# Third-norm cluster logits: the row block as stationary side, the centroids as 128 and 64 moving columns

## The reference, cut to what matters

```
x = x + 0.5 * ffn(layernorm(x))
x = x + attention(layernorm(x))
x = x + 0.5 * ffn(layernorm(x))

def ffn(x):                                   # x: 4096 x 1024
    dots = softmax(x @ centroids.T / 0.1)     # 64 centroids of 1024 features
    hits = dots > 0.01
    query_sel   = any(hits, axis=1)           # per token
    cluster_sel = any(hits, axis=0)           # per cluster
    row_sel = cluster_sel[assignments]        # per output feature
    dense = x @ weight.T + bias               # 1024 x 1024 weight
    return where(query_sel[:, None] & row_sel[None, :], dense, 0)
```

## Time and profile before

| what | value |
|---|---|
| median of 3 runs | 1194.87 us (1193.89 to 1196.8) |
| time of the profiled execution | 1196.15 us |
| its span in the trace | 1194.3 us |
| PE busy | 1181.7 us (99%) |
| PEld busy | 1002.5 us (84%) |
| DVE, ACT, POOL busy | 799.3, 499.2, 441.0 us |
| granted TensorE clock over the span | 1.00 |

### The profile page before, as it was taken

One profiled execution on the slowest core, in us unless ns is written; L12 is line 12 of the kernel. 1 busy time (PEld: TensorE's weight loads), 2 busy tenths in 40 slices (PEclk: granted clock), 3 DMA queues, 4 the chain that ended last, 5 costly groups with the idle time before them and its releaser, 6 DMA issues.

```text
span 1194.3 us, 24986 instructions
## 1 busy us (share of the span) xinstructions
PE 1181.7 (99%) x10072; PEld 1002.5 (84%) x10072; DVE 799.3 (67%) x1272; ACT 499.2 (42%) x718; POOL 441.0 (37%) x582
## 2 busy tenths in 40 slices
PE   7999999999999999999999999999999999999998
PEld 6888888888888888888888888888888878888887
DVE  6654554455444477787777877778777774199987
ACT  5232233222211355656656656565565663211110
POOL 1335445543424643433434334344343210051332
PEclk9999999999999999999999999999999999999999
DMA  8578777876565366565565666565655565017885
GB/s 275 144 206 232 207 206 193 225 211 182 164 189 159 98 169 169 148 171 146 160 166 139 181 152 152 160 155 164 161 142 164 129 169 193 2 72 259 279 304 195
DMA packets 344978, 208.73 MB, mean 175 GB/s; under 512 B 289440, under 2 KB 308640, under 8 KB 344864
## 3 DMA queue, kind: packets, MB, share of 16 engines
q1 hardware_dynamic: 329696, 187.73, 56.2%
q10 hardware_dynamic: 15168, 19.40, 4.7%
HBM read 118.49 MB, written 88.60 MB: 173 GB/s over the span
## 4 chain that ended last, share of the span: by engine, by line
PE 91%; DMA 3%; DVE 2%; issue 1%; ACT 1%; SPq 1%; POOL 1%; POOLq 0%; DVEq 0%
PE ps_b L285 9%; PE ps_q L285 8%; PE ps_q L287 8%; PE ps_q L286 8%; PE ps_b L287 8%; PE ps_b L286 8%; PE ps_a L285 8%; PE ps_a L287 8%; PE ps_a L286 8%; PE ps_t L292 6%; PE ps_q L1450 3%; PE ps_q L299 2%; PE ps_q L301 2%; PE ps_q L1425 2%; DMA y_scratch<-xa 1%
## 5 line engine op out<-in xcount | busy, mean ns | idle before, releaser
L318 POOL TENSOR_TENSOR var_eps<-moments,eps 128x1 f32<-128x1 f32 x96 | 18.2, 190 | 396.6 <-DVE moments L314 396.6
L285 PE MATMUL ps_a<-w_hi,odd_hi 128*128 128x512 f32 x368 | 147.7, 401 | 0.0
L287 PE MATMUL ps_a<-w_hi,odd_lo 128*128 128x512 f32 x368 | 143.8, 391 | 0.0
L286 PE MATMUL ps_a<-w_lo,odd_hi 128*128 128x512 f32 x368 | 143.2, 389 | 0.0
L635 POOL TENSOR_SCALAR f_out<-f_out,token_on 128x1024 f32<-128x1024 f32 x30 | 85.6, 2852 | 75.6 <-DVE f_out L1013 75.3
L686 POOL TENSOR_TENSOR x_ring<-x_ring,f_tmp 128x1024 f32<-128x1024 f32 x32 | 77.3, 2414 | 91.2 <-DVE best L1159 58.5
L285 PE MATMUL ps_b<-proj_hi,y_hi 128*128 128x512 f32 x256 | 103.3, 403 | 0.0
L287 PE MATMUL ps_b<-proj_hi,y_lo 128*128 128x512 f32 x256 | 100.0, 391 | 0.0
L286 PE MATMUL ps_b<-proj_lo,y_hi 128*128 128x512 f32 x256 | 99.7, 390 | 0.0
L327 ACT ACTIVATE y_tok<-x_ring,norms 128x1024 f32<-128x1024 f32 x64 | 79.7, 1245 | 38.0 <-ACT o_head L881 21.0
L737 POOL TENSOR_TENSOR late<-late,mask 128x1024 f32<-128x1024 f32 x18 | 44.1, 2463 | 137.3 <-DMA late<-x_scratch 91.6
(11 more groups left out here) (219 smaller groups left out, 3113.1 us busy)
## 6 DMA issues: line engine op xcount, KB each, us to landing
xa<-in_L_attn_x SPq DMA_DIRECT2D x32, 512.0 KB, 5.0
f_tmp<-f_scratch SPq DMA_DIRECT2D x32, 512.0 KB, 4.2
x_ring<-in_L_attn_x SPq DMA_DIRECT2D x32, 512.0 KB, 3.6
f_scratch<-f_out SPq DMA_DIRECT2D x30, 512.0 KB, 4.0
x_scratch<-x_ring SPq DMA_DIRECT2D x30, 512.0 KB, 3.5
y_scratch<-xa SPq DMA_DIRECT2D x28, 512.0 KB, 4.6
ya_tok<-y_scratch SPq DMA_DIRECT2D x112, 128.0 KB, 3.3
late<-x_scratch SPq DMA_DIRECT2D x22, 512.0 KB, 6.7
```

The source lines that it names most:

```text
L285: pe.matmul(acc, hi[:, k, :], w_h[:, k, cols], start=(k == 0), stop=False)
L286: pe.matmul(acc, hi[:, k, :], w_l[:, k, cols], start=False, stop=False)
L287: last = pe.matmul(acc, lo[:, k, :], w_h[:, k, cols], start=False, stop=(k == KB - 1))
```

## The change

For the pairs of the third norm, pair_logits gives way to a new function, token_logits. It takes the 128 tokens of one block as stationary side: for each of the 2 blocks and 8 slices one matmul with the high token part stationary and all 128 centroid columns moving, and one with the low token part stationary and the 64 high centroid columns moving. The sums come out as tokens x centroids, written to logit_at(u). The copy by ScalarE and the two transposes fall away, and VectorE waits for pair_done in place of folded. The pairs of the first norm stay as they are.

```diff
+        def token_logits(pe, u):
+            at = logit_at(u)
+            for n in range(2):
+                for k in range(KB):
+                    hi, lo = odd_hi[:, k, n, :], odd_lo[:, k, n, :]
+                    if k == KB - 1:
+                        pe.matmul(at[:, n * P:n * P + NCL], lo, cen[:, k, 0:NCL], start=False, stop=False)
+                    last = pe.matmul(at[:, n * P:(n + 1) * P], hi, cen[:, k, :], start=(k == 0), stop=(k == KB - 1))
+                    if k < KB - 1:
+                        pe.matmul(at[:, n * P:n * P + NCL], lo, cen[:, k, 0:NCL], start=False, stop=False)
+            return last
...
-            dve.wait_ge(folded, u + 1)
+            if u >= NP:
+                dve.wait_ge(pair_done, u + 1)
+            else:
+                dve.wait_ge(folded, u + 1)
...
-                    if 0 <= i - 4 < NT - 2 and i % 2 == 1:
-                        copy_pair(NP + (i - 4) // 2)
...
-                copy_pair(2 * NP - 1)
...
-                        pair_logits(pe, odd_hi, odd_lo).then_inc(pair_done, 1)
+                        token_logits(pe, u).then_inc(pair_done, 1)
...
-                    if 0 <= i - 4 < NT - 2 and i % 2 == 1:
-                        fold_pair(NP + (i - 4) // 2)
...
-                pair_logits(pe, odd_hi, odd_lo).then_inc(pair_done, 1)
+                token_logits(pe, 2 * NP - 1).then_inc(pair_done, 1)
...
-                fold_pair(2 * NP - 1)
```

## The result

The changed kernel takes 1221.49 us (median of 4 runs, 1219.39 to 1226.04) against 1195.84 us for the kernel before (4 runs). The ratio is 1.022, with a 95% interval of 1.0184 to 1.0255. Run again on the chip of the first experiments it took 1222.51 us against 1194.69, ratio 1.0243 (1.0214 to 1.0272). The prediction was 1218 us, in a range of 1203 to 1250, from a change of +22.6 us; the measured change is +25.7 us.

The account below looks back on a forecast made before the run. The prediction took TensorE to bound the kernel: 56.3 us added less 33.7 us removed gave +22.6 us, so 1218.8 us from the profiled execution or 1217.5 by the median, written as 1218 us, range 1203 to 1250.

Parts of the forecast that it names:

- The bound: TensorE bounds the edited stretch, idle once for 0.9 us from 560 to 1060 us; every microsecond on it moves the end.
- rival D: Added work fills TensorE's idle time, at most 0.9 us; chance 0.02, shared with a cancelling mixture of two other rivals.
- The added term: Third-norm logits on TensorE: 32 narrow matmuls a pair at 0.110 us, the load's price; 56.3 us over 16 pairs.
- The removed terms: Off TensorE in the third norm: centroid-stationary logits, 29.9 us, and two transposes a pair, 3.8 us; 33.7 us in all.
- ScalarE's copy and VectorE's wait: Third norm: the copy, 0.37 us, was under cover, and VectorE's earlier softmax in the last pair, some 3 us, gains nothing.
- A: Third-norm narrow matmuls pay more than their load, such as moving columns too; net +43 us, 1239 us; chance 0.20.
- B: Loads of the third-norm narrow matmuls overlap in part, 0.082 us each; net +8 us, 1204 us; chance 0.09.
- C: Loads of the third-norm narrow matmuls are hidden, only moving columns count; net -6.3 us, 1190 us; chance 0.09.
- sign of being wrong: The odd iteration growing by other than 1.2 to 1.8 us, or a TensorE wait at the later scores or select_count.

Follow-up runs that it names:

- e1: Changed kernel with the low matmuls moving all 128 centroid columns in place of 64; 1217.05 us, ratio 1.0188 to the kernel before.
- e2: Changed kernel with only the first 64 tokens of the block as stationary side in the low matmuls; 1204.08 us, ratio 1.008 to the kernel before.
- e5: Changed kernel with each of the 512 narrow matmuls moving 256 columns, the 128 centroid columns twice; 1222.93 us.
- e3: Kernel before without the copy and the two transposes in the third norm; 1191.87 us, ratio 0.998.

## Why the prediction was right

*The bound.* TensorE had 0.9 us of idle time in the edited stretch before and has 0.2 us of it now. The prediction put the whole edit behind 560 us and asked that nothing change ahead of it; that was a misreading, since three pairs lie there, and it changed nothing in the sum. Everything put on TensorE came out at the end, so rival D is out.

*The added term.* 32 matmuls a pair were priced at 0.110 us, 3.52 us a pair, 56.3 us. The trace has 3.52 us, to the hundredth. The value came from the transposes' row and from the difference of two load records, and e1, e2 and e5 show that the reason was right too: the stationary columns pay, and a matmul costs 0.110 us with 64 and 128 moving columns in turn, 0.110 with 128 and 0.120 with 256. Since 0.110 was the price of a neighbouring row and 0.108 to 0.120 were its bounds, the hit to the hundredth owes something to luck; that the load is what counts does not. The 81 ns that the Trainium skill gives in "TensorE: Matmul & The Clock Gate", section "Back-to-back issue gap", for a stream of loads and 128-column matmuls appear in no run here with 128 stationary columns in each. The same page's rule for the load, in section "LDWEIGHTS (loading the stationary operand)", 107 ns for 128 columns, agrees with the 0.110.

*The removed terms.* 1.87 and 0.22 us a pair stand against a measured difference of the iterations of 2.11 us, and e3 puts the fold at 0.21. The odd iteration grew by 1.46 us, not by 3.52 - 2.11 = 1.41; 0.03 of the difference lies in the transposes behind the logits, which hold the chain of waits of the changed kernel for 0.90 us in place of 0.87:

```profile
627.34 0.90 PE ps_t L292 x8
```

The sum of +22.6 us comes out, without dips, as 16 x 1.46 = +23.4 in the profile and as +22.4 in e1_low_128.

*ScalarE's copy and VectorE's wait.* No wait of TensorE took their place. In the last pair VectorE now reads the logits right behind its low part, with no idle time, where it had waited 2.90 us:

```profile
1057.68 0.28 DVE L353 COPY pair_exp_in<-ps_q 128x128 f32<-128x128 f32 x1
```

The hits are ready at 1061.14, 6 us before TensorE asks for them at 1067.19, and nothing was won, as predicted.

*Rivals.* A is refuted by e1 and e5, B and C by the beat of the loads.

*What was missed.* The forecast held the granted clock at full for good. It had no term for the dips, which cost about 1.6 us each (one 2 us) and up to 11 us an execution. In the iterations that have one the odd iteration grew by 3.1 to 3.5 us, outside the 1.2 to 1.8 that the prediction named as its sign of being wrong. They are enough for the 3.5 us by which the median lies above the forecast. They also go with the scatter, 7 us where the kernel before has 4, though not with all of it: two runs at the same mean clock of 0.994 took 1222.74 and 1226.04 us. They were outside the reasoning, and that the time stayed inside the range all the same is no merit of the reasoning.

## What to carry to other kernels

On a TensorE-bound kernel, count for each matmul the longer of two things, its own moving columns and the stationary columns of the next load. Here 128 stationary columns cost 0.110 us and 256 moving ones 0.120, so the operand with fewer columns belongs on the stationary side, even at the price of a copy and two transposes (3.8 us here). A load-bound stretch of narrow matmuls can bring the clock down: look at the granted clock at its end and behind it, not only inside it.

## What the hardware showed that was not expected

The granted clock fell to half at the end of 3.5 us of matmuls that moved 64 and 128 columns in turn, with TensorE busy in every microsecond of the dip. It did so at every second pair over a part of two executions, 4 and 7 times, and the mean clock stayed at 1.000 in the 4 runs in which the low matmuls moved 128 columns at the same beat. The Trainium skill, in "TensorE: Matmul & The Clock Gate", section "What's actually happening", says that the gate follows how busy the engine has been and knows a half and a full rate. The trace agrees on the two levels (0.50 and 1.00). It does not agree if busy means what the records call busy: they give TensorE 1.00 of every microsecond from 586 to 592 us. What in the work the clock answers to, why one pair in two is hit, and why some executions have more of it, stays open.

So a kernel can gain by computing more: with a third more moving columns e1_low_128 took 1217.05 us against 1222.51.
